# Gated cross-attention layer with a routed FFN: the rounding of the weighted middle rows on ScalarE instead of VectorE

## What is computed

```
x = x + tanh(g_xattn) * attention(layernorm(x), ctx, masks, Wq, bq, Wk, bk, Wv, bv, Wo, bo)
y = layernorm(x)
probs = softmax(y @ router_w)                      # 16 experts
weights, idx = top_k(probs, 2); weights = weights / sum(weights)
combine = sum of weights * one_hot(idx)            # tokens x 16
g = y @ gate_w[e];  u = y @ up_w[e];  h = silu(g) * u     # 96 middle rows per expert
x = x + tanh(g_ffn) * sum over e of (h @ down_w[e]) * combine[:, e]
```

## Time and profile before

| what | value |
|---|---|
| median of 3 runs | 252.52 us (252.23 to 252.58) |
| profiled execution | 252.51 us |
| its span | 250.6 us |
| PE busy | 224.0 us (89%) |
| DVE busy | 174.2 us (70%) |
| ACT busy | 94.0 us (37%) |
| POOL busy | 96.5 us (38%) |

### The profile page before, as it was taken

How to read it: one execution, slowest core, us unless ns; L and a number is a source line. 1 busy time by engine, 2 the same in 40 slices (tenths; PEclk the granted TensorE clock), 3 DMA queues, 4 the chain that set the end, 5 groups by cost and what they waited for, 6 DMA issues and landing times.

```text
span 250.6 us, 3685 instructions
## 1 busy us (share of the span) xinstructions
PE 224.0 (89%) x1219; PEld 158.9 (63%) x1219; DVE 174.2 (70%) x354; ACT 94.0 (37%) x175; POOL 96.5 (38%) x129
## 2 busy tenths in 40 slices
PE   0876498989999999999598899989999999999993
PEld 0752263565555555556334688778888879898992
DVE  2668768648777878776933566948978687775665
ACT  2465157656566665746445521011101010101000
POOL 6356424400608393920811020401999633520000
PEclk9999689999999999999979999999999999999998
DMA  6371611007760302020042000013455521223104
GB/s 202 80 225 31 157 32 24 0 0 166 172 151 19 68 0 63 0 65 0 0 114 84 30 12 1 3 51 122 104 130 130 176 94 43 67 61 83 43 3 167
DMA packets 26274, 18.62 MB, mean 74 GB/s; under 512 B 15600, under 2 KB 22320, under 8 KB 26256
## 3 DMA queue, kind: packets, MB, share of 16 engines
q1 hardware_dynamic: 25952, 18.17, 27.1%
q10 hardware_dynamic: 304, 0.22, 0.4%
HBM read 14.15 MB, written 1.11 MB: 61 GB/s over the span
## 4 chain that ended last, share of the span: by engine, by line
PE 69%; DVE 13%; POOL 6%; DMA 4%; issue 2%; ACT 1%; SPq 1%; ACTq 0%; DVEq 0%; POOLq 0%
PE bank L1006 60%; DVE mneg L869 2%; PE bank L1046 2%; DMA wkv_n<-in_L_xattn_Wv 2%; POOL cT L547 2%; PE bank L1063 2%; POOL cT L546 2%; POOL w_d L551 2%; PE bank L1067 1%; POOL w_d L550 1%; DMA w_t<-comb_d 1%; DVE cb L915 1%; DVE q L941 1%; DVE pT L937 1%; DVE x_sb L999 1%
## 5 line engine op out<-in xcount | busy, mean ns | idle before, releaser
L1006 PE MATMUL bank<-xT,cT 128*128 128x512 f32 x288 | 70.1, 393 | 0.3 <-DVE pT L929 0.3
L1006 PEld LDWEIGHTS bank<-xT,cT 128*128 128x128 f32 x288 | 52.6, 188 | 11.8 <-issue 0.8
L869 DVE TENSOR_REDUCE mneg<-bank 128x4 f32<-128x512 f32 x64 | 43.1, 685 | 14.5 <-PE bank L1006 13.6
L688 ACT ACTIVATE pT<-bank 128x512 f32<-128x512 f32 x64 | 38.2, 599 | 24.6 <-PE bank L1006 23.5
L675 ACT ACTIVATE pT<-bank 128x512 f32<-128x512 f32 x24 | 14.4, 598 | 77.2 <-PE bank L1006 77.2
L1006 PE MATMUL bank<-q,kz 112*128 112x512 f32 x64 | 38.9, 610 | 0.0
L1006 PE MATMUL bank<-w_d,q 128*128 128x256 f32 x288 | 38.5, 284 | 0.3 <-DVE q L943 0.3
L1006 PEld LDWEIGHTS bank<-w_d,q 128*128 128x128 f32 x288 | 37.0, 190 | 2.6 <-issue 1.2
L929 DVE TENSOR_TENSOR pT<-pT,bank 128x512 f32<-128x512 f32 x24 | 16.4, 684 | 21.7 <-PE bank L1006 20.1
L1006 PE MATMUL bank<-kz,q 96*128 96x512 f32 x64 | 26.7, 426 | 4.8 <-DVE mneg L869 3.2
L1006 PE MATMUL bank<-ident_b,cmask 128*128 128x512 bf16 x64 | 25.4, 397 | 1.2 <-ACT q L609 1.2
(11 more groups left out here) (125 smaller groups left out, 277.3 us busy)
## 6 DMA issues: line engine op xcount, KB each, us to landing
w_t<-comb_d SPq DMA_DIRECT2D x16, 192.0 KB, 2.9
w_t<-comb_d SPq DMA_DIRECT2D x16, 128.0 KB, 2.9
padf<-in_L_ffn_down_w SPq DMA_DIRECT2D x12, 128.0 KB, 2.2
c_sb<-in_ctx SPq DMA_DIRECT2D x2, 512.0 KB, 6.5
q<-cT SPq DMA_DIRECT2D x8, 128.0 KB, 2.8
w_t<-comb_d SPq DMA_DIRECT2D x16, 64.0 KB, 2.7
out<-x_sb SPq DMA_DIRECT2D x4, 256.0 KB, 2.4
q<-xn SPq DMA_DIRECT2D x8, 96.0 KB, 2.2
```

What stands on the lines that cost most here:

```text
L688: nc.scalar.activation(pT[:, i // 4, i % 4, :], bank[2 + s % 2][:], ACT.Exp, scale=SCALE).then_inc(p_done, 1)
L869: nc.vector.tensor_reduce(mneg[:, r, 4 * hf:4 * hf + 4], bank[SQ_BANK[n % 3]][:].rearrange("p (g k) -> p g k", g=4), X, ALU.max, negate=Tr ...
L1006: return nc.tensor.matmul(dst, a, b, start=start, stop=stop, skip_group_check=True)
```

## The change

ACT gets a new function `hidden_high(n)`, which copies h_all into hh and increments a new semaphore hh_ok. `weigh(n)` on DVE keeps the multiplication alone; `hidden_low(n)` waits for hh_ok and does the subtraction. Both of DVE's parts are called where weigh was. ACT calls `hidden_high(n)` in the slots of WEIGH_SLOT, behind the slot's normalisation and ahead of its Silu, and in a tail loop hidden_high(n+1) ahead of silu(n+3).

```diff
+        hh_ok = sem("hh_ok")
...
+            def hidden_high(n):
+
+                sc.wait_ge(rep_used, n + 1)
+                if n == 0:
+                    sc.wait_ge(st_done, CH)
+                if n >= 2:
+                    sc.wait_ge(y_done, 2 * (n - 1))
+                nc.scalar.copy(hh[:, n % 2], h_all).then_inc(hh_ok, 1)
+
...
                         normalise(NQ + b, b)
+                for n, at in WEIGH_SLOT.items():
+                    if s == at:
+                        hidden_high(n)
                 for n, at in UP_SLOT.items():
                     if s == at + 1:
                         silu(n)
-            for n in range(len(UP_SLOT), len(ORDER)):
-                silu(n)
+            for n in range(len(DOWN_SLOT), len(ORDER)):
+                if n + 1 < len(ORDER):
+                    hidden_high(n + 1)
+                if n + UL < len(ORDER):
+                    silu(n + UL)
...
                 nc.vector.tensor_tensor(h_all, h_su[:, n % UL], c_rep[:, n % CR], ALU.mult).then_inc(rep_used, 1)
-                ve.wait_ge(rep_used, n + 1)
+
+            def hidden_low(n):
+
                 if n >= 2:
                     ve.wait_ge(y_done, 2 * (n - 1))
-                own(nc.vector.tensor_copy(hh[:, n % 2], h_all))
-                settle()
+                ve.wait_ge(hh_ok, n + 1)
                 nc.vector.tensor_tensor(hl[:, n % 2], h_all, hh[:, n % 2].bitcast(F32), ALU.subtract).then_inc(h_ok, 1)
...
                         weigh(n)
+                        hidden_low(n)
...
                     weigh(n + 1)
+                    hidden_low(n + 1)
```

## The result

The changed kernel takes 254.17 us (median of 4, 254.01 to 254.51), the kernel before 252.50 (median of 4): ratio 1.0070, 95% interval 1.0053 to 1.0087, so 0.5% to 0.9% slower. The forecast was 254.3. The profiled execution of the changed kernel took 254.51 us, with a span of 252.6: 2.0 more than the span before, while the medians are 1.7 apart.

A forecast was written before the change was run, and what follows sets the result against it. TensorE was taken as the bound, busy 77.5 of 77.8 us from 164.0. Terms 0.87 + 0.28 + 0.45 - 0.30 + 0.50 = +1.8 us on 252.5 gave 254.3, range 253.1 to 255.6.

The forecast's parts named there:

- The trip: From weighted tile to start of the low part via ACT: 0.75 us instead of 0.49, so 0.26 longer.
- Slot 70: Tile 1: down(1) starts 0.87 us late, bounds 0.49 to 1.14, and all later slots shift with it.
- ACT's order: In slot 70 the copy queues behind normalise(7), which waits for POOL's chain; part of the 0.87 us.
- POOL's relief: In slot 70 DVE's cast and subtraction move later, so rstd is ready at 148.99 instead of 149.26.
- Routing chain: Expert weights behind low(3) on DVE: the 0.26 us longer trip costs nothing, since POOL sets the end.
- The rival in which DVE gets in ahead: At the routing chain L911 starts before POOL's L546, saving at most 1.53 us: 252.8, no measurable change; 7%.
- Entry: Start of the dense stretch: down(4) 0.28 us later, then up(8) 0.45 more, with silu(7) behind tile 5's copy.
- The one wait in the dense stretch: TensorE's 0.30 us wait at 201.06 goes: -0.30 us, bound 0, and no more can be gained there.
- Steady rounds: nothing: Tiles 6 to 21, rounds of 4.18 us: copy and Silu are covered, so the edit costs nothing.
- the doubtful one: DMA-late tile 11, silu(13) behind weigh(11): argument for the rival of late Silu each round, 258.5 or 256.4; 6%.
- its list of signs of being wrong: CT(1) wait shrinking by over 1 us, a copy over 0.8, or TensorE waiting in the steady rounds.
- Drain: Tiles 22 and 23 at the end have no cover: two longer trips cost 0.50 us, bounds 0.45 to 0.9.

The follow-up runs named there:

- c1: Changed kernel with ACT's copy ahead of the last batch's normalisation in slot 70; 253.66 us, ratio 1.0052 to the kernel before.
- d2: Changed kernel with an extra DVE cast and subtraction from SBUF while DVE waits for ACT's copy of tile 1; 254.68 us, ratio 1.0083.
- d3: Changed kernel with two extra DVE maxima over SBUF while DVE waits for ACT's copy of tile 1; 254.60 us, ratio 1.0085.
- c2: Changed kernel with silu(n+3) ahead of hidden_high(n+1) in ACT's tail loop; 253.91 us, ratio 1.0057 to the kernel before.
- f3: Changed kernel with copy ahead of normalisation, silu ahead of copy, and DVE casting the last two tiles; 253.28 us, ratio 1.0025.
- d1: The changed kernel itself, measured again on another occasion; 254.43 us, ratio 1.0087 to the kernel before.
- f2: Changed kernel with ACT copying only tiles 6 to 20, silu ahead of the copy, slot 70's order unaltered; 252.54 us, ratio 0.9983.
- f1: The version of d4, measured again on another occasion; 252.01 us, ratio 0.9969 to the kernel before.
- c4: Changed kernel with DVE's own cast for tiles 22 and 23; 253.81 us, ratio 1.0052 to the kernel before.
- d4: Changed kernel: ACT copies only tiles 1, 6 to 20; copy before normalisation, silu before copy; tile 1's subtraction awaits POOL; 251.79 us, ratio 0.9968.

## Why the prediction was right, and where its sizes were off

- **The trip:** 0.75 was forecast; DVE idles 0.76 (copy 0.619, the hand-over back 0.10). Right.
- **Slot 70:** 0.87 forecast, 0.81 in the ledger; POOL's chain took the 1.80 us forecast, and c1, d2 and d3 show both parts of the argument, ACT's order and POOL's relief. Right.
- **Routing chain:** forecast as covered by POOL, and B is unchanged (13.66 against 13.67). DVE's L927 (the old L911) took 0.81 in place of 1.07 and ended with POOL's operation again. The rival in which DVE gets in ahead did not come about: L927 starts 0.26 after POOL's operation, and TensorE still waits 1.28 us for comb. That wait is 0.25 shorter than before because down(3) now starts 0.25 later, behind low(3); this is how the 0.26 is covered.
- **Entry:** 0.28 and 0.45 forecast, 0.27 and 0.58 measured; the hand-over from Silu to up(8) was 0.14, the upper end (175.61 to 175.75), and the round behind it was 0.06 longer. c2 shows that this cost is ACT's order, f3 that the first is the trip's.
- **The one wait in the dense stretch:** the term that was mis-sized. The step took TensorE's 0.30 of idle time in the earlier trace rows for the whole and said that more could not be gained there; by milestones the round from down(10) to down(11) lasts 4.78 us in place of 4.18, 0.60 more. The changed kernel gets 0.61 back in its second profile, but 0.19 in its first, where this round takes 4.60. "Steady rounds: nothing" failed at this one tile, which the text had named as the doubtful one, and a TensorE wait in these rounds was on its list of signs of being wrong. The rows of the first profile:

```profile
198.51 1.43 DVE L953 TENSOR_TENSOR pT<-pT,w_t 128x512 f32<-128x512 f32 x1 [2.27 <-DMA w_t<-comb_d]
...
199.97 0.62 ACT L679 CAST q<-pT 128x512 fp32r<-128x512 f32 x1 [5.24 <-DVE pT L953]
200.50 0.59 ACT L685 ACTIVATE pT<-bank 128x512 f32<-128x512 f32 x1
...
201.24 3.00 PE L1025 MATMUL bank<-xT,cT 128*128 128x512 f32 x12 [0.17 <-POOL cT L548]
```

  The copy of tile 11 stands ahead of silu(13) behind a late weigh; Silu ends at 201.09, and up(14) starts 0.15 later. (The row names POOL's split, which ends at 201.10; in d1 up(14) starts 0.64 ahead of the end of that split, so it does not need it.) What differs between the two cases is when the DMA with the combine weights of tile 11 lets weigh(11) start. In all eight profiles of kernels with the copy on ACT where it starts 1.15 us or more ahead of down(10), the round is 4.17 to 4.19; with 0.96 (and 1.43 us for the multiplication beside POOL) it is 4.60. Where Silu stands ahead of the copy, late weights cost less: the round is 4.34 with 0.52 (f2), 4.45 with 0.11 (f1) and 4.46 with 0.08 (c2). The cast itself also counts: the kernel before, with the weights 0.48 and 0.63 ahead, loses 0.60 both times, and f2, with them 0.52 ahead and the copy on ACT, loses 0.16. Why the DMA comes earlier in one execution than in another was not followed.
- **Drain:** 0.50 forecast, 0.51 measured; c4 takes it away.

The sum came out at 1.8 against a measured 1.7. The mechanisms held, but that it is so near is in part luck: the gain in the dense stretch was taken too small against the second profile (0.30 for 0.61) and too large against the first (0.19), and the cost at the entry was 0.13 too small.

## What to carry to other kernels

When a short step is moved to an idle engine, count the trip (here 0.76 us from the data to the next step, for a 0.43 us cast) only where nothing covers it, and look at what stands ahead of the step in the other engine's queue: about half of the loss here was one copy behind a normalisation that waited for a third engine. Split such a change by stage: in the one dense round where a cast stretched beside POOL held up TensorE, the move helps, and in the others it costs nothing; at the ramp and in the drain, where the chain is bare, the engine that has the data should keep the step. A ledger of fixed milestones on the bounding engine sizes a stage to a few hundredths of a microsecond where whole-kernel times scatter by 0.3% and more; a stage that waits on a DMA (E here) needs more than one profile.

## What the runs showed of the hardware that was not expected

The idle time shown for TensorE can be less than what a wait costs: 0.30 us in the row and 0.60 in the round in the kernel before, 0.17 and 0.42 in the changed one, and in f1 none at all and 0.27. The rows show one part of the reason: in an unbroken run twelve 128x512 matmuls are shown with 2.91 us, but the next group starts 2.75 after them (d4: 198.40, 2.91, then 201.15), so a wait must use up this 0.16 before idle time is shown. What makes up the rest stays open.

POOL's small operations on 128x1 operands depend on what DVE does beside them: one went from 0.19 to 0.65 us beside a DVE subtraction with two SBUF operands (c1), and none was longer beside 1.28 us of DVE maxima over SBUF with one operand (d3).
